# Row maxima of layer one by DMA instead of matmul and copy, scores half a head earlier

## The reference

```python
q = _split_heads(hidden_states @ Wq.T, H)
k = _split_heads(text @ Wk.T, H); v = _split_heads(text @ Wv.T, H)
out_text = _merge_heads(_attend(q, k, v, sm_scale))
k_ip = _split_heads(ip @ Wk_ip.T, H); v_ip = _split_heads(ip @ Wv_ip.T, H)
out_ip = _merge_heads(_attend(q, k_ip, v_ip, sm_scale))
out = (out_text + IP_SCALE * out_ip) @ Wo.T + bo + residual
```

## Time and profile before

| | us |
|---|---|
| median of 3 runs | 1715.8 |
| lowest and highest | 1711.35 and 1715.96 |
| the profiled execution, its own time | 1714.97 |
| its span, first to last instruction | 1713.2 |
| PE busy in the span | 1586.2 (93%) |
| VectorE busy | 1277.6 (75%) |
| ScalarE busy | 1113.8 (65%) |
| GpSimd busy | 441.6 (26%) |

### The profile page before, as it was taken

The page is one execution under the profiler, slowest core; times in us unless marked ns, Lnnn a source line. Parts: engine busy times, 40 slices in busy tenths (PEclk is TensorE's granted clock), DMA queues, the critical chain, the costliest instruction groups (busy, mean ns, idle before and its releaser), DMA issues.

```text
span 1713.2 us, 26860 instructions
## 1 busy us (share of the span) xinstructions
PE 1586.2 (93%) x8608; PEld 1211.7 (71%) x8608; DVE 1277.6 (75%) x3548; ACT 1113.8 (65%) x2323; POOL 441.6 (26%) x1233
## 2 busy tenths in 40 slices
PE   6888999999988899999998889999998889999993
PEld 3554489999455459999755537999965544899991
DVE  2797378887789538888779835888877982788875
ACT  1797367775399547777459926777727972677760
POOL 0343023322044112233114402333203430232320
PEclk9999999999999999999999999999999999999996
DMA  9010310010411230001221032000031103000100
GB/s 311 24 37 15 111 58 21 20 35 1 123 39 37 59 95 25 20 20 30 54 83 37 29 91 69 20 21 22 22 111 39 37 15 111 14 22 22 34 2 16
DMA packets 47780, 83.62 MB, mean 49 GB/s; under 512 B 4868, under 2 KB 12308, under 8 KB 47640
## 3 DMA queue, kind: packets, MB, share of 16 engines
q1 hardware_dynamic: 44968, 76.77, 14.6%
q10 hardware_dynamic: 2672, 5.13, 0.9%
HBM read 41.49 MB, written 34.10 MB: 44 GB/s over the span
## 4 chain that ended last, share of the span: by engine, by line
PE 77%; ACT 16%; issue 2%; DVE 1%; DMA 1%; SPq 1%; POOL 0%; DVEq 0%; ACTq 0%
PE ps_w L938 46%; PE ps_s L938 12%; PE ps_t L938 11%; PE ps_b L938 7%; ACT probsT_high L522 5%; ACT probsT L530 5%; ACT probs L541 3%; ACT q_slots L515 3%; PE ps_m L938 1%; DMA q_slots<-out_all 1%; DMA q_slots<-probsT_low 1%; SPq L350 0%; ACT probs L618 0%; POOL probsT_low L433 0%; SPq L312 0%
## 5 line engine op out<-in xcount | busy, mean ns | idle before, releaser
L714 DVE TENSOR_TENSOR probsT_low<-probsT,probsT_high 128x512 fp32r<-128x512 f32 x560 | 397.5, 710 | 80.4 <-ACT probsT L530 76.3
L522 ACT ACTIVATE probsT_high<-ps_t 128x512 fp32r<-128x512 f32 x640 | 382.3, 597 | 114.1 <-PE ps_t L938 112.1
L938 PE MATMUL ps_w<-gram,probsT_high 128*128 128x416 f32 (+2 forms) x1280 | 388.1, 314 | 0.0
L530 ACT ACTIVATE probsT<-ps_t 128x512 f32<-128x512 f32 x640 | 384.1, 600 | 0.0
L938 PE MATMUL ps_w<-gram_low,probsT_high 128*128 128x384 f32 (+2 forms) x1280 | 352.0, 303 | 0.0
L453 POOL TENSOR_SCALAR exp_bias<-row_max 128x1 f32<-128x1 f32 x320 | 123.4, 385 | 695.9 <-DVE row_max L772 695.9
L558 ACT ACTIVATE probs<-ps_s,exp_bias 128x508 f32<-128x508 f32 x320 | 218.9, 685 | 123.5 <-POOL exp_bias L453 85.9
L938 PE MATMUL ps_t<-q_slots,k_slots 98*128 98x512 f32 x640 | 256.3, 421 | 0.9 <-ACT probsT L530 0.5
L938 PEld LDWEIGHTS ps_w<-gram_low,probsT_high 128*128 128x128 f32 (+1 forms) x1280 | 243.0, 190 | 10.9
L938 PEld LDWEIGHTS ps_w<-gram,probsT_high 128*128 128x128 f32 (+1 forms) x1280 | 241.0, 188 | 9.1
L938 PE MATMUL ps_w<-gram,probsT_low 128*128 128x400 f32 (+2 forms) x1280 | 245.4, 314 | 0.0
(11 more groups left out here) (166 smaller groups left out, 2011.6 us busy)
## 6 DMA issues: line engine op xcount, KB each, us to landing
q_slots<-parts_q SPq DMA_DIRECT2D x128, 96.0 KB
k_slots<-parts_k SPq DMA_DIRECT2D x128, 96.0 KB
parts_k<-probsT_high SPq DMA_DIRECT2D x16, 512.0 KB, 4.4
parts_k<-probsT_high SPq DMA_DIRECT2D x24, 256.0 KB, 4.3
parts_q<-probsT_low SPq DMA_DIRECT2D x8, 512.0 KB, 3.8
parts_q<-x_sb SPq DMA_DIRECT2D x8, 512.0 KB, 4.6
k_slots<-probsT_high SPq DMA_DIRECT2D x24, 128.0 KB, 3.9
parts_q<-probsT_low SPq DMA_DIRECT2D x12, 256.0 KB, 4.2
```

Source lines behind the costliest of these rows:

```text
L522: nc.scalar.activation(probsT_high[1 - par][:, t, :], ps_t[:, t % 2, :], ACT.Exp, scale=SCALE)
L530: nc.scalar.activation(probsT[:, t, :], ps_t[:, t % 2, :], ACT.Exp, scale=SCALE).then_inc(pt_block[l], 1)
L714: nc.vector.tensor_tensor(probsT_low[1 - par][:, t, :], probsT[:, t, :], probsT_high[1 - par][:, t, :].bitcast(F32), ALU.subtract).then_in ...
L938: return nc.tensor.matmul(out, lhsT, rhs, start=start, stop=stop)
```

## The change

- `head_maxT` and `shift` of layer one are gone. VectorE writes the maxima of a head into `row_max[0]` as two groups of four numbers per partition, and SP sends each group by DMA into row 96 or 97 of the slot: 128 pieces of 16 bytes, 2 KB, two DMAs per head. For this the four numbers of a partition must be neighbours in the row, so chunk c of layer one's scores is no longer queries 128c to 128c+127 but every fourth query from c on; the weights of these products are read with a stride of four elements.
- The scores stand half a head earlier: step n makes half 1 of head n+2 and half 0 of head n+3. The code of VectorE moves alike. Layer one's PE now waits for the rows (`rows_in`) before the transposed block 0, and VectorE waits for the rows of head n+1 before it overwrites its maxima with those of head n+3.
- Query and key slots are one tensor, `slots`, and one scratch tensor per layer: a slot is filled by one DMA of 192 KB, in both layers, whose source runs over columns first and then parts. The order of the 48 rows changes accordingly.
- SP's queue takes the row DMAs between the slot loads, and the store of the batch before goes behind all of layer one's slot loads.

```diff
-SLOT_LOADS = 2 * 16
+SLOT_LOADS = 16
+SHIFTS = SHIFT_ROWS * 16
...
-        scratch = {n: nc.dram_tensor(f"parts_{n}", [3, TURNS, D, SLOTS, S], F32, kind="Internal").ap()
-                   for n in ("k0", "q0", "k1", "q1")}
+        scratch_of = [nc.dram_tensor(f"parts{l}", [3, TURNS, D, SLOTS, 2, S], F32, kind="Internal").ap() for l in range(2)]
+        scratch = {f"{n}{l}": scratch_of[l][:, :, :, :, i, :] for l in range(2) for i, n in enumerate("qk")}
...
-                for slot, src in ((q_slot[k], scratch[f"q{l}"]), (k_slot[k], scratch[f"k{l}"])):
-                    sp.dma_start(slot[0:SCORE_ROWS, :].bitcast(F32), src[:, turn, :, k, :])\
-                        .then_inc(slots_in[l][k], 16)
+                sp.dma_start(slots[0:SCORE_ROWS, k, :, :].bitcast(F32),
+                             scratch_of[l][:, turn, :, k, :, :].rearrange("p d i s -> d p i s")).then_inc(slots_in[l][k], 16)
...
+            def shift(b, n, k):
+
+                sp.wait_ge(max_half, 2 * (HEADS * b + n + 1) + CREDIT)
+                for r in range(SHIFT_ROWS):
+                    sp.dma_start(q_slots[SHIFT_ROW + r:SHIFT_ROW + r + 1, k, :].bitcast(F32),
+                                 row_max[0][k % 2][:, r, :].bitcast(F32)).then_inc(rows_in[k], 16)
...
-                if scores:
-                    shift(b, 0, n + 1, k + 1)
...
-                if scores:
-                    maxima0(b, n + 2, 1, par)
+                if scores_next and not first:
+                    rows_loaded(dve, b, k + 1, turn)
+                    maxima0(b, n + 3, 0, 1 - par)
...
-            def scores_chunk(slot, c, out):
-
-                return mm(out, q_slot[slot][0:FULL_ROWS, P * c:P * c + P], k_slot[slot][0:FULL_ROWS, :], True, True)
+            def scores_chunk(l, slot, c, out):
+
+                q = q_slot[slot][0:FULL_ROWS, :].rearrange("r (p c) -> r c p", c=SC)[:, c, :] if l == 0 else \
+                    q_slot[slot][0:FULL_ROWS, P * c:P * c + P]
+                return mm(out, q, k_slot[slot][0:FULL_ROWS, :], True, True)
...
                 if transposed:
+                    rows_loaded(pe, b, k + 1, turn)
                     scoresT_of(0, g, k, 0)
...
-                if scores:
-                    scores_half(1)
+                if scores_next and not first:
+                    scores_half(3, 0)
...
-                if scores:
-                    pe.wait_ge(max_half, 2 * (g + 3) + CREDIT)
-                    head_maxT(0, par)
```

More of the change, by code:

```diff
@@ L218, in build @@
         low_last = sem("low_last")
-        maxT_done = [sem(f"maxT_done{l}") for l in range(2)]
-        shift_in = [sem(f"shift_in{l}") for l in range(2)]
+        maxT_done = sem("maxT_done")
+        shift_in = sem("shift_in")
+        rows_in = [sem(f"rows_in{i}") for i in range(SLOTS)]
         gram_high = sem("gram_high")
@@ L368, in split_and_loaded @@
                     store(name, m)
-                if l == 0 and b is not FIRST:
-                    store_outputs(b)
+                if l == 0:
+                    shift(batch, 0, 0)
+                    shift(batch, 1, 1)
                 for name in names:
@@ L376, in split_and_loaded @@
                         load_slots(batch, l, turn + 1, k)
+                        if l == 0:
+                            shift(batch, SLOTS * turn + k + 2, (k + 2) % SLOTS)
+                if l == 0:
+                    for k in range(2, SLOTS):
+                        shift(batch, HEADS - SLOTS + k, k)
+                if l == 0 and b is not FIRST:
+                    store_outputs(b)
+            def shift(b, n, k):
[3 more added lines that the diff above has]
+                                 row_max[0][k % 2][:, r, :].bitcast(F32)).then_inc(rows_in[k], 16)
             def store_outputs(b):
@@ L410, in _, with step0 @@
                                     pattern=[[-1, P]], channel_multiplier=1).then_inc(built, 1)
-            def step0(b, n, k, turn, use, transposed, scores, last=FIRST):
+            def step0(b, n, k, turn, use, transposed, scores, scores_next, last=FIRST):
                 par = k % 2
@@ L1025, in step0 @@
                     wait_freed(pe, last, "q0", 2)
+                if first:
+                    scores_half(2, 0)
+                    values0(last)
                 if scores:
-                    scores_half(0)
-                if first:
-                    values0(last)
+                    scores_half(2, 1)
                 if output:
```

77 lines of the change are left out of this document (43 added, 34 removed).

## The result

The changed kernel takes 1696.8 us (median of 6 runs, 1693.2 to 1701.6) against 1715.6 before: a ratio of 0.9895, 95% interval 0.9874 to 0.9917, 18.8 us less. Kernels of different series are compared by their ratios to the kernel before, which ran in every series. The forecast was 1682, with a range of 1667 to 1705.

The account below looks back on a forecast made before the run. It took ScalarE's chain with the row shift to bound layer one's 5.45 us step: 68 x (5.45 - 4.94) = 34.7 us less, 1.4 more for the fill, from 1715.0 to 1681.7, run median 0.8 above: 1682 us, range 1667 to 1705.

Parts of the forecast that it names:

- What goes: Layer one's step loses the shift, 0.75 us of ScalarE's chain, and four ps_m products on PE, 0.24 us.
- ScalarE's circle alone: ScalarE's own chain of waits over one layer-one step, without the shift: 5.45 - 0.75 = 4.70 us.
- The three circles: Chains closed over one layer-one step: VectorE's queue 4.77 us, ScalarE's first exponentials 4.76, PE's order between the halves 4.74.
- VectorE's circle: VectorE's queue in layer one's step, from half 0's big maximum to the next, scores' latency included: 4.77 us.
- h: Extra time per half of layer one's scores for the strided weight load: 0.10 us taken, upper bound 0.34.
- PE's circle: PE's order between layer one's score halves: 4.74 us, with both strided halves 4.94, taken as the step.
- Rival 1: Layer one's strided load costs near its bound: steps of 5.24 to 5.42 us, 1702 to 1714 us; chance 0.12.
- L: Time from the end of the maximum to the second row's landing in the slot: 2.45 us.
- the two-step form (L + 6.18) / 2: Step length from the rows' circle, closed over two layer-one steps: 4.32 us for L = 2.45, 4.94 at L = 3.7.
- Rival 2: The 16-byte row pieces land late: at L = 6 the step is 6.09 us, the kernel 1759 us; chance 0.10.
- The fill: First batch's start: the rows' landing replaces some 1.1 us before the transposed block, costing 1.4 us once.
- the marks named ahead: Expected profile: intervals about 4.9 us, no q_slots<-ps_m, VectorE or PE in ScalarE's place, VectorE near 98% busy, loads 200-260 ns.

Follow-up runs that it names:

- experiment 5: Kernel before with layer one's scores half a head earlier and ps_m products ahead of the new half; shift and loads kept: 1749.7 us, ratio 1.0195.
- experiment 3: experiment 1's kernel with VectorE's subtraction of block 1 cut to 128 of 512 columns from a batch's third head on: 1677.0 us, ratio 0.9773.
- experiment 1: Changed kernel with layer one's score weights read contiguously, maxima still in strided order, so output differs: 1689.7 us, ratio 0.9839.
- experiment 6: Changed kernel with the scores back in the order of before, maxima still sent by DMA: 1817 us (one run).
- experiment 7: Changed kernel with four more DMAs of a head's maxima issued ahead of the two real ones: 1761.7 us (one run).
- experiment 8: Kernel before with queries and keys side by side, one 192 KB load per slot, in both layers: 1714.6 us, ratio 0.9992.
- experiment 10: experiment 2's kernel with block 1's subtraction on GpSimd, 1681.7 us; plus busy products and output projection ahead in later fills, 1681.0; without busy products, 1678.0.
- experiment 9: Changed kernel with 13 products that nobody reads set into PE's waits in the first batch's fill: 1700.3 us, ratio 0.9902.
- experiment 2: Changed kernel with score weights at a stride of 8 bytes and maxima sent by halves, four row DMAs a head: 1693.4 us, ratio 0.9859.
- the first kernel of experiment 10: experiment 2's kernel with layer one's block 1 subtraction moved from VectorE to GpSimd and nothing more: 1681.7 us, ratio 0.9793.

## Why the prediction was right, and where it was off

- **What goes.** Right. The shift and the ps_m products left the chain, and that ScalarE had held the step fits experiment 5, which keeps the shift and gains nothing. The forecast of 4.70 for ScalarE's circle alone was never reached: once VectorE is relieved (experiment 3), the step is 4.76, in a circle of PE's products and four exponentials in which ScalarE still waits 0.29 us for a transposed block.
- **The three circles.** The step that failed is "All three say about 4.77", in which VectorE's circle had 0.06 until PE may overwrite ps_s and 0.67 until the new scores are there. Both were read where they didn't apply: they are 0.15 and, without the stride, 0.80. The rows split the 0.80. Before, a pair of score products takes 0.63, and VectorE starts 0.04 after it (1318.32 + 0.63 = 1318.95, then 1318.99). In experiment 1 it takes 0.70, and VectorE starts 0.10 after it (1306.89 + 0.70 = 1307.59, then 1307.69). The 0.07 is the weight load: it ran during earlier products, and stands in the open now that PE waits for the maximum with this half too. The other 0.06 and the 0.09 go with a second semaphore wait. PE has one for the slot ahead of this pair (`max_half,slots_in00`), VectorE one for the rows (`s_half,rows_in2`). No run changed a wait by itself, but the traces separate it. In the fills, shown below, pairs behind the wait for the maximum alone start 0.06 after its end (59.12 in the change, behind 58.01 + 1.05, and 53.42 before, behind 52.31 + 1.05); pairs behind two waits start 0.15 and 0.16 after it (51.86 behind 50.66 + 1.05, 54.16 behind 52.95 + 1.05). And in experiment 5, where VectorE has no rows to wait for, it still starts 0.03 after the pair (1326.80 + 0.68, then 1327.51). 4.77 + 0.13 + 0.09 = 4.99, as measured without the stride.
- **The strided load.** The mechanism was right; h measured 0.13, where 0.10 was taken. But I let PE's circle rule, which carries it twice (4.94), and VectorE's rules, which carries it once: 4.77 + 0.22 + 0.13 = 5.12, 0.18 over the forecast. My doubling as upper bound was fair: a load went from 188 to 319 ns. Rival 1, with steps from 5.24 on, did not occur.
- **The row DMAs.** L of 2.45 measured 0.47 + 0.04 + 1.99 + 0.04 = 2.54 in experiment 6. The cover is real: experiment 6 takes it away and a step takes 6.12, experiment 7 uses it up and the two-step form (L + 6.18) / 2 holds with 6.4 for 6.18. Rival 2 did not occur: PE waits four times for the rows in the whole kernel, 1.8 us in all.
- **One load per slot at nothing.** Right (experiment 8).
- **The fill.** Forecast 1.4 us once, for the landing alone; it is 5.3 in the first batch and 8.1 over the three others, which I had costed at nothing. The term that was missing is the move's. PE's rows of the first fill, before and then in the change:

```profile
48.88 0.86 PE L938 MATMUL ps_s<-k_slots,q_slots 96*128 96x512 f32 x2
...
52.20 0.73 PE L938 MATMUL ps_t<-q_slots,k_slots 98*128 98x512 f32 x2 [0.16 <-ACT q_slots L515]
53.42 0.74 PE L938 MATMUL ps_s<-k_slots,q_slots 96*128 96x512 f32 x2 [0.49 <-DVE row_max L729]
```

```profile
49.51 0.88 PE L963 MATMUL ps_s<-slots 96*128 96x512 f32 x2
51.86 0.82 PE L963 MATMUL ps_s<-slots 96*128 96x512 f32 x2 [1.48 <-DVE row_max L748]
54.16 0.82 PE L963 MATMUL ps_s<-slots 96*128 96x512 f32 x2 [1.47 <-DVE row_max L748]
54.82 0.81 PE L963 MATMUL ps_t<-slots 98*128 98x512 f32 x2
...
59.12 1.24 PE L963 MATMUL ps_s<-slots 96*128 96x512 f32 x2 [0.60 <-DVE row_max L748]
```

  The scores start 0.63 later. From them to the first transposed block it is 5.31 us instead of 3.32: one more half of scores, for which PE waits 1.47 us, now stands ahead of it, and the landing hides behind that. With the DMA alone (experiment 6) the same stretch is 4.82, 1.5 more than before and near the forecast of 1.4; with the move alone (experiment 5) it is 5.18. The last 2.65 lie behind the block, where the granted clock has a mean of 0.69 in 52 to 60 us and 0.67 in 60 to 68, and 1.00 in the kernel before. In the later batches it is again a half of scores that waits 1.47 us for the maxima of the one just ahead; experiment 10 removes that wait. In the third gap the clock fell too (0.79 in 1276 to 1284).
- **What offset it.** 3.0 us from the last two steps of the batches, and 5.0 at the end, which the sum had at zero. The 5.0 is luck as far as the runs show: the mean clock over the last 73 us is 0.84 after and 0.79 before, and 0.76 in experiment 9's kernel, which has the same code there and takes 4.1 us longer.
- **The sum.** 22.7 of 34.7 us from the steps; fills -13.4, last steps and end +8.0: 17.3 for the two profiled executions. The medians are 18.8 apart.
- Of the marks named ahead, the missing q_slots<-ps_m and PE in the chain in ScalarE's place came as said. The interval was 5.12, not about 4.9. VectorE "near 98% busy" was wrong, 46.7 of 51.2 us: its circle includes the time in which it waits for scores. Loads of 200 to 260 ns were wrong too, 319.

Open: what makes the clock fall in the first fill. It fell there in the change and in experiments 5, 6 and 9 (to means of 0.50 to 0.60 in the lowest 8 us of 52 to 68, 0.67 in the change), and stayed at 1.00 before and in experiment 8. PE's waits just ahead of it are not needed for it, by experiment 9.

## What to carry to other kernels

A latency read in the profile belongs to the state of its queue: if the change makes an engine wait at a place where its next operands used to be loaded in advance, add the load, and add what the waits themselves cost: a second semaphore wait ahead of an instruction went with 0.06 to 0.09 us here, on PE and on VectorE. When several circles come out within a few per cent, the chain of waits won't tell which one rules; shortening one engine's row in one run, and moving one instruction in another, did, and an innocent-looking move ahead of the ruling engine's queue cost 0.56 us a step. Two halves of a change can each be a loss and the pair a gain: the DMA alone made the step 6.1 to 6.9 us, the move alone 5.74, both together 5.12. And what two single traces differ by in a fill or at the end may be the clock's doing: look at a third kernel with the same code there before you count it.

## What the hardware showed

- A weight load of 96x128 in fp32r takes 188 ns contiguous, 195 at a stride of 8 bytes, 319 at 16.
- A copy of 128 pieces of 16 bytes from 128 partitions into one lands 2.0 us after its issue when SP issues two together (median; 1.8 to 3.6 in the change); of 8 bytes, four together, 2.3 (1.8 to 3.4 in experiment 2, up to 4.0 in the first kernel of experiment 10). Its issue holds SP 0.52 us with two and 0.60 with four together (medians; 0.47 at least).
- PE starts a pair of products 0.06 us after the maximum that it waited for when this wait stands alone, and 0.15 to 0.16 after it behind two waits. VectorE starts 0.03 to 0.04 after the pair's end with one wait and 0.10 with two (experiments 1 and 5).
- TensorE's clock fell to its lower level, 1.2 GHz, after 8 us in which PE was busy 7.94 (experiment 9), as it did in the change with PE busy 6.53 of the 8; in the kernel before, with PE busy 6.62, it stayed at the upper level, 2.4 GHz.
